# Cross attention on one core: another order of VectorE's work in a slot, and three pieces of the prologue at other places

## What is computed

```python
q = _heads(hidden_states @ to_q_w)                       # 20 heads of 16
h_txt = _sdpa(q, _heads(ehs_txt @ to_k_w), _heads(ehs_txt @ to_v_w))
h_obj = _sdpa(q, _heads(ehs_obj @ to_k_object_w), _heads(ehs_obj @ to_v_object_w))
h_oth = _sdpa(q, _heads(ehs_oth @ to_k_others_w), _heads(ehs_oth @ to_v_others_w))
h_ip = _sdpa(q, _heads(ehs_ip @ to_k_ip_w), _heads(ehs_ip @ to_v_ip_w))
out = _merge(h_txt) + _merge(h_obj) + _merge(h_oth) + _merge(h_ip)
out = out @ to_out_w + to_out_b
out = out + residual
```

## Time and profile before

| | |
|---|---|
| median of 3 runs | 1812.3 us |
| lowest and highest | 1810.25 and 1822.74 us |
| the profiled execution | 1827.61 us |
| its span, first to last instruction | 1825.8 us |
| mean granted clock of TensorE | 0.979 |
| TensorE matmuls busy | 1690.6 us, 93% |
| VectorE busy | 1495.5 us, 82% |
| GpSimd busy | 1249.3 us, 68% |
| ScalarE busy | 1040.9 us, 57% |

### The profile page before, as it was taken

One profiled execution on the slowest core, in us unless ns is written; L12 is line 12 of the kernel. 1 busy time (PEld: TensorE's weight loads), 2 busy tenths in 40 slices (PEclk: granted clock), 3 DMA queues, 4 the chain that ended last, 5 costly groups with the idle time before them and its releaser, 6 DMA issues.

```text
span 1825.8 us, 48271 instructions
## 1 busy us (share of the span) xinstructions
PE 1690.6 (93%) x15120; PEld 1383.0 (76%) x15120; DVE 1495.5 (82%) x3536; ACT 1040.9 (57%) x1860; POOL 1249.3 (68%) x1452
## 2 busy tenths in 40 slices
PE   6859999999999999999999999999999999999987
PEld 3547777788777778777777877777787777787765
DVE  4148988988888888888898888889888888888897
ACT  1135666665565566565666656566665655665564
POOL 3237677767766766777776777677677767767644
PEclk9979999999999999999999999999999999999999
DMA  7678987887888787888788788878878887877861
GB/s 281 171 201 194 222 199 208 214 205 211 206 212 198 204 208 198 200 213 205 211 216 201 210 205 219 209 203 215 208 205 200 210 201 202 209 197 180 211 125 37
DMA packets 409172, 366.24 MB, mean 201 GB/s; under 512 B 17137, under 2 KB 380210, under 8 KB 404786
## 3 DMA queue, kind: packets, MB, share of 16 engines
q1 hardware_dynamic: 409138, 365.79, 79.5%
HBM read 216.30 MB, written 149.42 MB: 200 GB/s over the span
## 4 chain that ended last, share of the span: by engine, by line
PE 67%; DVE 17%; issue 8%; ACT 4%; DMA 1%; DVEq 0%; SPq 0%; ACTq 0%; POOL 0%; POOLq 0%
PE job_ps L786 28%; PE ring_ps L852 10%; PE ring_ps L872 8%; PE ring_ps L865 7%; DVE l_seg L667 6%; PE s_ps L825 4%; PE job_ps L802 4%; DVE probs L640 4%; DVE rest L657 2%; DVE m_seg L624 2%; PE ring_ps L753 2%; ACT probs L543 2%; PE job_ps L796 1%; PE job_ps L805 1%; ACT parts L525 1%
## 5 line engine op out<-in xcount | busy, mean ns | idle before, releaser
L463 POOL TENSOR_TENSOR probs<-probs,rl 128x616 f32<-128x616 f32 (+1 forms) x640 | 628.8, 1005 | 362.6 <-DVE rl L678 357.6
L786 PE MATMUL job_ps<-c_in,w_kv 128*128 128x172 f32 (+1 forms) x2560 | 576.9, 368 | 22.0 <-DVE rest L657 22.0
L552 ACT ACTIVATE pT<-ring_ps 128x512 f32<-128x512 f32 x640 | 378.3, 598 | 356.8 <-PE ring_ps L852 348.2
L786 PEld LDWEIGHTS job_ps<-c_in,w_kv 128*128 128x128 f32 x2560 | 424.5, 190 | 111.2 <-DVE rest L657 29.7
L667 DVE TENSOR_REDUCE l_seg<-probs 128x8 f32<-128x616 f32 (+1 forms) x640 | 385.8, 645 | 56.3 <-ACT probs L543 56.3
L852 PE MATMUL ring_ps<-ident,probs 128*128 128x128 f32 x2560 | 389.4, 277 | 9.3 <-DVE y L687 8.0
L640 DVE TENSOR_TENSOR probs<-s_ps,m_seg 128x616 f32<-128x616 f32 (+1 forms) x640 | 387.3, 647 | 0.0
L624 DVE TENSOR_REDUCE m_seg<-s_ps 128x8 f32<-128x616 f32 (+1 forms) x640 | 368.9, 618 | 0.0
L543 ACT ACTIVATE probs<-probs 128x1024 f32<-128x1024 f32 x320 | 337.5, 1055 | 15.8 <-DVE probs L644 15.8
L852 PEld LDWEIGHTS ring_ps<-ident,probs 128*128 128x128 f32 x2560 | 290.4, 143 | 64.5 <-issue 25.4
L657 DVE TENSOR_TENSOR rest<-job_ps,parts 128x512 f32<-128x512 f32 (+1 forms) x192 | 130.7, 681 | 144.6 <-ACT parts L525 144.6
(11 more groups left out here) (47 smaller groups left out, 1402.9 us busy)
## 6 DMA issues: line engine op xcount, KB each, us to landing
q_all<-q_scratch SPq DMA_DIRECT2D x64, 960.0 KB, 8.5
k_all<-k_scratch SPq DMA_DIRECT2D x64, 960.0 KB, 12.7
c_in<-in_cT SPq DMA_DIRECT2D x32, 1024.0 KB, 5.0
x_raw<-in_xT SPq DMA_DIRECT2D x32, 768.0 KB, 4.4
q_scratch<-parts SPq DMA_DIRECT2D x64, 384.0 KB, 3.0
k_scratch<-parts SPq DMA_DIRECT2D x64, 384.0 KB, 2.5
x_res<-in_x SPq DMA_DIRECT2D x128, 160.0 KB, 3.4
out<-y SPq DMA_DIRECT2D x128, 160.0 KB, 2.9
```

The source lines that it names most:

```text
L463: pool.tensor_tensor(pr[:, :, a:e], pr[:, :, a:e], r[:, :, s:s + 1].broadcast_to((P, OH, e - a)), ALU.mult)
L552: act.activation(pT[:, h:h + QH, :], ring_ps[i][:, :].rearrange("p (h s) -> p h s", h=QH), ACT.Copy)\
L786: last = pe.matmul(dst[:, :, a:e], w_kv[:, l, k, i * P:(i + 1) * P], c_in[:, k, :, a:e], start=(k == 0), stop=(k == CK - 1))
```

## The change

Four edits. In VectorE's slot the remainders of jobs that ended at place 1 now stand, like those of place 0, ahead of the shift: maxima, outputs, remainders of both places, shift, sums, reciprocals. In the prologue TensorE makes the scores of octets 0 and 1 ahead of the last early job (kv2 of turn -1) and VectorE their first maxima ahead of that job's remainder; as probs shares its space with the small jobs' results, which the last early job reads, VectorE waits for all early jobs before the first shift. ScalarE rounds the third x behind the first two spreads of v, and GpSimd takes its x_low behind all splits of the prologue.

```diff
@@ GpSimd, prologue @@
                 x_low(1, k)
             for n in range(3, NSP):
                 split(0, n)
-            for n in range(3):
+            for n in range(NSP):
                 split(1, n)
             for k in range(CX):
                 x_low(2, k)
-            for n in range(3, NSP):
-                split(1, n)
@@ ScalarE, prologue @@
                 evacuate(turn, job)
-                if job == ("q", 2):
+                if (turn, job) == (-2, ("q", 2)):
                     for k in range(CX):
-                        x_high(turn + 3, k)
+                        x_high(1, k)
             spread(0, 0)
             spread(0, 1)
+            for k in range(CX):
+                x_high(2, k)
@@ VectorE, prologue @@
+                if (turn, job) == EARLY_JOBS[-1]:
+                    reduce_max(0, 0)
                 if job in SPLITS:
                     subtract_part(turn, job)
 
             dve.wait_ge(small_stored, 16)
-            reduce_max(0, 0)
+            dve.wait_ge(job_filled, len(EARLY_JOBS))
             shift(0, 0)
@@ VectorE, slot @@
-                for turn, job in ended(g, n - 1, 0):
-                    if job in SPLITS:
-                        subtract_part(turn, job)
+                for at in range(2):
+                    for turn, job in ended(g, n - 1, at):
+                        if job in SPLITS:
+                            subtract_part(turn, job)
                 if live(gg, G):
                     shift(gg, o)
                 if live(g, G):
                     sum_up(g, n)
-                for turn, job in ended(g, n - 1, 1):
-                    if job in SPLITS:
-                        subtract_part(turn, job)
-                if live(g, G):
                     invert(g, n)
@@ TensorE, prologue @@
+                if (turn, job) == EARLY_JOBS[-1]:
+                    pe.wait_ge(small_freed, N_SMALL)
+                    pe.wait_ge(w_o_loaded, 16 * 3)
+                    for o in range(2):
+                        scores(0, o)
                 work(turn, job)
-            pe.wait_ge(small_freed, N_SMALL)
-            pe.wait_ge(w_o_loaded, 16 * 3)
-            for o in range(2):
-                scores(0, o)
```

## The result

| | before | after |
|---|---|---|
| median (runs taken together) | 1816.97 us (4) | 1750.43 us (4) |
| lowest and highest | 1810.25 and 1822.74 us | 1748.99 and 1752.15 us |
| profiled execution | 1827.61 us | 1750.32 us |
| its span | 1825.8 us | 1748.5 us |

The ratio after to before is 0.9635, with a 95% interval from 0.9593 to 0.9678: faster. The forecast was 1750.0 us. The profiled spans differ by 77.3 us, where the terms of the sum add up to 78.0.

What follows compares the result with a forecast made beforehand. TensorE was taken as the bound, back to back except for waits on VectorE's remainder subtractions. 1827.6 - 58.8 (wait before q2) - 18.8 (clock falls) - 0.4 (prologue) = 1749.6, stated as 1750 us; range 1742 to 1772.

Steps and rivals of the forecast that it cites:

- q2's wait: TensorE's idle time before q2, until VectorE subtracts q1's remainder, goes to nothing: 30 x 1.96 = 58.8 us, lower end 51.6.
- The step "For q1, ...": VectorE can subtract q1's remainder from 840.7 to 841.4, so the bank is free before TensorE needs it for q2.
- the step on q2: q2 and ScalarE's copy of it come 1.96 us earlier; VectorE arrives at about 845.3 and has no wait.
- The clock: TensorE's 12 clock falls behind the idle time before q2, 1.57 us each, go: 18.8 us of gain.
- The second sum, from the median: Median 1812.3 us taken to hold some two clock falls: 1812.3 - 3.5 - 59.2 = 1749.6 us.
- VectorE's slack: On VectorE, up to the remainder of kv0, 0.4 us a group is left after the change: enough, but thin.
- The rival in which VectorE is the bound: VectorE becomes the bound between slot 2 and slot 8; losing 1 us more a group gives 1780 us; chance 0.08.
- The new waits: VectorE waits for ScalarE's copies of kv1 (1.5 us) and kv2 (0.4 us) in slots 9 and 0; cost 0.
- kv1's own wait: TensorE's wait before kv1 for the remainder of kv0 stays 0.68 us; value 0.
- The prologue: TensorE's hole before about 108 us stays, set by a store landing at 106.6; earlier first scores gain 0.4 us.
- The sum: Profiled execution 1827.6 us less 58.8, 18.8 and 0.4 gives 1749.6 us, stated as 1750.

Runs made afterwards that it cites:

- q1 alone: Changed kernel with only q1's remainder ahead of the shift, those of q2, kv1 and kv2 behind the sums again: 1792.86 us, ratio 0.9875.
- the filled gap: Kernel before with 16 more transpositions on TensorE in the idle time in front of q2, result unchanged: 1810.32 us, ratio 0.996.
- the added subtractions: Changed kernel with one or two more VectorE subtractions in front of q2's remainder in each group: 1755.11 us with one, 1772.4 us with two.
- the early stores: Changed kernel with the stores of q0, q1 and q2 of turn -1 ahead of four loads on SyncE: 1736.9 us, ratio 0.9559.
- all but q1's: Changed kernel with q1's remainder behind the sums again, those of q2, kv1 and kv2 ahead of the shift: 1810.45 us, ratio 0.9993.

## Why the prediction was right, point by point

- **q2's wait (58.8 us).** Right in size: 57.5 us over 29 groups, and it went in the first group too. (The 1.92 us that stand in that group in front of q1, at 138.62, are another wait, which the edit leaves.) Of the two ends of its price, the weight loads' 1.96 us and the matmuls' 1.72, the first was right: 1.98 to 1.99 a group. I had weighed there that TensorE may pull a weight load ahead of running matmuls (Trainium skill, TensorE: Matmul & The Clock Gate, section "Architectural detail: the array is 16× 32×32, not 1× 128×128"). These traces agree with the page once the bank is free: the load starts at 553.86, ahead of the end of the transpositions at 554.13. While it waited for the bank it was not ahead of anything, and so the higher end was the price: q2's start came 1.96 us nearer to the transpositions.
- **The reason given for it was incomplete.** The step "For q1, ..." credited the whole gain to q1's remainder, and the step on q2 said only that its move costs no wait. q1 alone gave 0.57 us of 1.99, for kv0 then waits for q2's bank. The time forecast is right because the change moves both. The rows of before could have shown it: with q2 1.96 us sooner, kv0 comes sooner too, and in the old order q2's remainder would have stood behind a shift and sums, 2.5 us in the earlier trace rows. I followed the wait removed, and not the next use of a bank behind it.
- **The clock (18.8 us).** Right: 12 falls went, all 200 us stretches of the steady part are at 1.00 (the next fall, at 1695 us, is in the tail, where before has its own), and the filled gap shows that idle time was the cause. One fall came in, in the first group behind a 1.92 us stall that the change doesn't touch, 1.6 us. The section "HAM oscillation — how this bites in real kernels" of the same page of the Trainium skill, by which stalls between bursts of matmuls bring the half rate back, agrees in direction. It tells of waits of 3 to 5 us; what the runs add is that stalls of 1.72 us did so in some groups and not in others, and that 1.16 us (one trace) and 0.68 us never did in the steady part of these traces.
- **The median.** The second sum, from the median, was no second check: its 3.5 us are the difference 1812.3 - 1808.8 itself, so it had to come out at the 1749.6 of the first. No run here shows that the median run had two falls. What carries the forecast is the time without falls, and it holds: before varies with its falls from set to set, and the sets beside the experiments had medians from 1814.3 to 1825.2 us and runs up to 1831.5, with none below 1808.5.
- **VectorE's slack** of 0.4 us a group: 0.36 us of wait left ahead of kv0's remainder, 0.47 by the added subtractions. The rival in which VectorE is the bound was less than one subtraction away.
- **The new waits** for kv1 and kv2, forecast at 1.5 and 0.4 us: 1.44 and 0.36, no cost; even 120.7 us of such waits in one kernel cost nothing.
- **kv1's own wait** stayed at 0.68 us, as said.
- **The prologue.** The hole stays and ends with the store's landing, as said, and the early stores show that it is the cause. Of the gain of 0.4, 0.5 is there at the first scores (120.40 against 120.87), but kv1 of before stood at 108.03 and now at 108.18, and the kernels with and without the prologue edits agree at 1748.7 without the fall: too small to be told from nothing.
- **The sum**: 78.0 forecast and 77.3 found, since the fall that came in (-1.6) and the first kv1 (-0.15) take back what the rest had more.

## What to carry to other kernels

When an engine works in order, put what frees a buffer ahead of the long work that nobody waits for yet, and then ask at once what the next use of a freed buffer will wait for: here one of the two moves that carry the gain gave under a third of it alone, and the other alone nothing. A hole may have two causes of one length; taking one away shows as a new releaser in front of the same hole, and that row names the next edit. A stall of under 2 us per group can cost nearly as much again in a fallen clock, in some runs and not in others, so count the slow groups in the trace before comparing medians.

## What the runs showed of the hardware

- Behind an idle time of 1.72 us TensorE's granted clock fell to the 1.2 GHz level in 12, 4 and 11 groups of three traces (before, the prologue edits alone, all but q1's) with the same idle time in every group, and each fall cost 1.57 us. Behind the 1.92 us in the first group it fell in six of thirteen traces. The falls come in rows of groups, mostly (5 and 7 in before's trace, 9 and 2 in the trace of all but q1's). What sets when such a row begins stays open.
- The landing of one and the same store differed with its place: the 128 KB one of q0 took 8.1 us when issued at 98.51, behind the loads, and 5.1 us when issued some 13 us sooner, ahead of them (the kernel with early stores). Whether the loads ahead of it or the other traffic of that time make the difference was not separated. The rest of the 15.9 us by which ScalarE's copy came sooner there is the place of the issue itself.
